# Mixing two of four batches as seven half-size products, with sums on VectorE and GpSimd

## The chip, the cores and the metric

The kernel runs on one core of one Trainium2 chip. TensorE does matrix products into PSUM, VectorE (DVE) and ScalarE (ACT) work on SBUF and PSUM, GpSimd (POOL) on SBUF alone, and SyncE (SP) issues the DMA transfers. The engines run their own instruction streams in order and wait for each other on semaphores. The metric is the device time of one execution in microseconds (us), the median over several runs.

## The reference

Four batches of 512 tokens, 512 model columns; context features of width 256, hidden width 2048.

```
query, key = ctx @ Wq.T + bq, ctx @ Wk.T + bk            # per batch, 512 x 128
A   = softmax(query @ key.T, axis=-1)                     # 512 x 512
x1  = x + tanh(g_xattn) * einsum('bln,bmn->blm', layernorm(x), A)
wu, wg, wd = ternary(W_up), ternary(W_gate), ternary(W_down)
out = x1 + tanh(g_ffn) * ((silu(layernorm(x1) @ wu.T) * (layernorm(x1) @ wg.T)) @ wd.T)
```

`layernorm` takes the mean and variance of a row; `ternary(W)` is round(W / mean|W|) clipped to -1, 0, 1, times mean|W|. The change is in the `einsum` of the third line, called the mix here: for each batch a 512 x 512 by 512 x 512 product in f32.

## The kernel before, in words

The program has an attention part (batches `b` = 0 to 3, the first 96 us) and a feed-forward part, which already multiplies in the scheme of seven half-size products. Every engine's order is written out by hand.

In batch `b`, TensorE projects the context of batch `b+1` (`project`), computes its attention energies (`energy`), transposes its softmax rows (`transpose_p`), and between these mixes batch `b` (`mix(b, i)`, `i` = 0 to 3, one for each 128 rows of tokens). A mix takes four 128 x 128 blocks of the transposed input `xT` (`xt_tile(i)`, loaded by `load_xt`) as weights and the transposed softmax `at_batch(b)` as 512 moving columns. Every f32 matmul is two records in the trace. The mix runs on the raw input. The row normalisation is put in afterwards: `stats1`/`aggregate1` on VectorE give mean and variance of the rows of `x`, `rstd1` on GpSimd turns them into the factor `tr1` (tanh(g) over the standard deviation) in four small steps, and `make_x1` on VectorE adds `tr1` times the mix to `x` and so frees the PSUM bank; there are two banks for the mix (`ps_x`).

Then `stats2`/`aggregate2` (VectorE), `rstd2` (GpSimd, two steps) and `norm_x1` (VectorE) normalise the result, and `high_t` (ScalarE) and `low_t` (VectorE) split it into two f16 parts, which DMA transposes carry to the feed-forward part. The blocks are called B11, B21, T3, T1, T2, B22 and T4; T3 to T4 are sums of blocks, that of T3 is the subtraction into `t3_sb`. In the same time ScalarE does for the next batch `bias_qk`, `exp_row`, `norm_p` (softmax rows divided by their sum) and `copy_at`, VectorE does `row_max` and `row_rsum`, and ScalarE also sums the absolute values of the weights as they land (`sum_abs`).

GpSimd's stream in this part holds the small steps only: `rstd1` and `rstd2` in the order of the tiles. A semaphore counts each kind of result: `s_r1` the rows whose `tr1` is there, `s_x1` the finished rows, `s_xm` the mixes, `s_at` the copied columns of the transposed softmax. `load_xt(b, i)` for batch 1 waits until `mix(0, i)` has read the buffer; the SP queue holds, in this order, `load_ug(1, 0)`, then `load_xt(1, 0)`, `load_ug(1, 1)`, `load_xt(1, 1)`, `load_ug(1, 2)`, `load_xt(1, 2)`, `load_ug(1, 3)`, `load_xt(1, 3)`, `load_x(2)`. `load_ug` brings a megabyte of feed-forward weights, `load_xt` a quarter of a megabyte.

## Time and profile before

| | |
|---|---|
| runs shown | 397.3, 398.37 and 398.42 us; median 398.37 |
| profiled execution, span from first to last instruction | 397.2 us |
| its own time | not listed beside the span; the median lies 1.2 us above the span |
| TensorE busy | 392.9 us, 99% of the span, granted clock 1.00 |
| VectorE, ScalarE, GpSimd busy | 309.2, 266.6, 153.5 us |
| attention part | until 96 us |

Busy time says how long an engine had an instruction in work. TensorE's records overlap, so its pace is read from the chain of waits: what ended last is followed back to what released it, and the chain's pieces follow each other without overlap. Idle time of an engine is listed with what ended it.

### The profile page before, as it was taken

What the parts mean: (1) busy time and instruction counts of PE and PEld (TensorE: products, weight loads), DVE (VectorE), ACT (ScalarE), POOL (GpSimd) and SP (SyncE); (2) the same over time, 40 slices, a digit from 0 to 9 for tenths busy, and PEclk for the clock granted to TensorE, in tenths of its full rate; (3) what the DMA queues carried; (4) which work ended last, traced back from release to release, by engine and by line L of the source; (5) the groups of instructions that cost most, each with busy time, mean ns of one, the idle gap of its engine ahead of it and who ended that gap; (6) DMA issues with size and microseconds to landing.
All of it is one profiled execution on the core that took longest, in us unless ns stands there. A gap on an engine that the chain in (4) does not pass through costs nothing.

```text
span 397.2 us, 5960 instructions
## 1 busy us (share of the span) xinstructions
PE 392.9 (99%) x1912; PEld 207.6 (52%) x1920; DVE 309.2 (78%) x457; ACT 266.6 (67%) x360; POOL 153.5 (39%) x189
## 2 busy tenths in 40 slices
PE   8999999999999999999999999999999999999997
PEld 6555545554444444444444444444445565656886
DVE  0666578988889986788897966686869989798974
ACT  3886898889779686868887863756277666654400
POOL 0224344657985004131338001535349556271000
DMA  7999949599610030030009543041500000000014
GB/s 268 410 420 390 376 173 224 141 248 217 134 70 1 2 106 2 0 106 2 1 2 212 110 90 68 0 146 70 173 37 2 0 2 1 2 0 2 0 55 160
DMA packets 43183, 43.91 MB, mean 111 GB/s; under 512 B 30992, under 2 KB 33168, under 8 KB 41104
## 3 DMA queue, kind: packets, MB, share of 16 engines
q1 hardware_dynamic: 43152, 43.53, 35.7%
q8 instruction: 16, 0.26, 0.3%
q14 instruction: 15, 0.12, 0.1%
HBM read 29.89 MB, written 6.29 MB: 91 GB/s over the span
## 4 chain that ended last, share of the span: by engine, by line
PE 93%; DVE 2%; issue 2%; ACT 1%; DMA 1%; POOL 0%; DVEq 0%; ACTq 0%; POOLq 0%
PE pair L718 23%; PE pair L720 22%; PE pair L650 14%; PE pair L792 14%; PE pair L836 11%; PE pair L625 4%; PE pair L611 3%; PE pair L636 2%; PE pair L665 1%; DMA xf<-in_first 1%; DVE xf L1467 1%; DVE x_sb L1518 0%; PE pair L669 0%; POOL xf L588 0%; DVE xf L1457 0%
## 5 line engine op out<-in xcount | busy, mean ns | idle before, releaser
L718 PE MATMUL pair<-xb_hi,w_sb 128*128 128x512 f16 x448 | 169.8, 379 | 0.2 <-DVE xf L1462 0.2
L720 PE MATMUL pair<-xb_lo,w_sb 128*128 128x512 f16 x448 | 169.8, 379 | 0.0
L718 PEld LDWEIGHTS pair<-xb_hi,w_sb 128*128 128x128 bf16 x448 | 43.8, 98 | 52.8 <-ACT xf L1145 0.9
L720 PEld LDWEIGHTS pair<-xb_lo,w_sb 128*128 128x128 bf16 x448 | 43.8, 98 | 51.1 <-issue 0.3
L1096 ACT ACTIVATE xf<-xf,small 128x512 f32<-128x512 f32 x48 | 34.6, 720 | 52.3 <-DVE xf L1462 31.6
L650 PE MATMUL pair<-sh,xt_sb 128*128 128x512 f32 (+2 forms) x160 | 57.4, 508 | 0.0
L792 PE MATMUL pair<-x_sb,sh 128*128 128x512 bf16 x248 | 55.1, 379 | 0.4
L1467 DVE SCALAR_TENSOR_TENSOR xf<-xf,small 128x512 f32<-128x512 f32 x48 | 40.0, 835 | 8.4 <-ACT xf L1096 8.4
L650 PEld LDWEIGHTS pair<-sh,xt_sb 128*128 128x128 f32 x160 | 28.0, 190 | 26.2 <-issue 22.0
L792 PEld LDWEIGHTS pair<-x_sb,sh 128*128 128x128 f16 x256 | 24.9, 98 | 30.6 <-DVE x_sb L1504 0.9
L512 POOL TENSOR_TENSOR w_sb<-w_sb 128x512 bf16<-128x512 bf16 x8 | 9.6, 1196 | 63.0 <-ACT w_sb L970 63.0
L1472 DVE TENSOR_TENSOR sh<-xf,sh 128x512 f16<-128x512 f32 x36 | 32.1, 897 | 0.7 <-ACT sh L1107 0.7
L1518 DVE SCALAR_TENSOR_TENSOR x_sb<-pair,small,x_sb 128x256 f32<-128x256 f32 (+1 forms) x57 | 25.5, 473 | 5.9 <-PE pair L836 5.4
L1504 DVE SCALAR_TENSOR_TENSOR x_sb<-pair,small,x_sb 128x512 f32<-128x512 f32 x32 | 23.9, 746 | 7.9 <-PE pair L792 7.7
L1107 ACT ACTIVATE sh<-xf 128x512 f16<-128x512 f32 x36 | 22.1, 623 | 10.5 <-DVE xf L1467 9.3
L584 POOL TENSOR_TENSOR xf<-xf 128x512 f32<-128x512 f32 x7 | 9.8, 1405 | 44.7 <-DMA xb_lo<-xf 28.7
L1457 DVE TENSOR_TENSOR xf<-pair,xf 128x1024 f32<-128x1024 f32 x16 | 19.5, 1221 | 8.8 <-PE pair L720 8.6
L1452 DVE TENSOR_TENSOR xf<-pair,xf 128x1024 f32<-128x1024 f32 x16 | 19.5, 1220 | 4.1 <-issue 1.6
L1462 DVE TENSOR_TENSOR xf<-pair,xf 128x1024 f32<-128x1024 f32 x16 | 19.5, 1219 | 4.1 <-PE pair L720 3.9
L1133 ACT ACTIVATE xf<-pair 128x1024 f32<-128x1024 f32 x16 | 16.4, 1023 | 8.1 <-PE pair L720 7.6
L1341 DVE SCALAR_TENSOR_TENSOR x_sb<-pair,small,x_sb 128x512 f32<-128x512 f32 x16 | 12.0, 747 | 11.3 <-PE pair L650 11.3
L1467 DVE SCALAR_TENSOR_TENSOR c<-c,small,pair 128x512 f32<-128x512 f32 x16 | 11.9, 743 | 10.1 <-ACT c L1096 10.1
(162 smaller groups left out, 654.6 us busy)
## 6 DMA issues: line engine op xcount, KB each, us to landing
w_sb<-in_wugT SPq DMA_DIRECT2D x8, 1024.0 KB, 11.3
xt_sb<-in_xT SPq DMA_DIRECT2D x16, 256.0 KB, 6.4
x_sb<-in_x SPq DMA_DIRECT2D x4, 1024.0 KB, 10.8
xf<-in_wdT SPq DMA_DIRECT2D x4, 1024.0 KB, 7.3
xt_sb<-in_wdT SPq DMA_DIRECT2D x4, 1024.0 KB, 5.2
x_dram<-x_sb SPq DMA_DIRECT2D x8, 256.0 KB, 2.8
out<-x_sb SPq DMA_DIRECT2D x8, 256.0 KB, 2.0
x_sb<-x_dram SPq DMA_DIRECT2D x2, 1024.0 KB, 5.7
```

The costliest lines, as they stand in the source:

```text
L650: last = pe.matmul(ps_x[i % 2][:, lo:hi], xt_tile(i)[:, k, :], at[:, k, lo:hi], start=(k == 0), stop=(k == KD - 1))
L718: pe.matmul(dst[:, m * 512:(m + 1) * 512], w[:, o:o + P], hi[:, k], start=start and k == 0, stop=False, skip_group_check=not start)
L720: last = pe.matmul(dst[:, m * 512:(m + 1) * 512], w[:, o:o + P], lo[:, k], start=False, stop=k == 1, skip_group_check=not start)
L792: ins = pe.matmul(dst, h_part(n, c, lo)[:, i * P:(i + 1) * P], t_d[:, e * DM + lo_col:e * DM + hi_col], start=first and n == units[0] and ...
L836: ins = pe.matmul(fin_bank(g, j, t), hidden(u, c, lo, min(t, NT - 1)), cols, start=first and u == units[0] and lo == 0 and not (side and t ...
L1096: act.activation(cb(n, c)[:, 0:512], src, ACT.Silu, scale=su[:, :]).then_inc(s_silu[c], 1)
L1107: act.activation(part(n, c, 0), shaped(n, c, cb(n, c)[:, 0:512]), ACT.Copy).then_inc(s_hi[c], 1)
L1452: dve.tensor_tensor(cb(n, "11"), ps_y[:, :], cb(n, "11"), ALU.add).then_inc(s_c["11"], 1)
L1467: dve.scalar_tensor_tensor(cb(n, c)[:, 0:512], cb(n, c)[:, 0:512], kap[:, :], gate, ALU.mult, ALU.mult).then_inc(s_mul[c], 1)
L1472: dve.tensor_tensor(part(n, c, 1), shaped(n, c, cb(n, c)[:, 0:512]), part(n, c, 0), ALU.subtract)\
L1504: dve.scalar_tensor_tensor(y_tile(b, i), at, c_out[:, :], y_tile(b, i), ALU.mult, ALU.add)\
L1518: dve.scalar_tensor_tensor(fin_rows(g, j, t), fin_bank(g, j, t), c_out[:, :], fin_rows(g, j, t), ALU.mult, ALU.add).then_inc(s_ef, 1)
```

## The change

In batches 0 and 1 (`NS` = 2) the mix is done as seven products of halves. The tokens are halved (`lh`), the columns of the attention matrix (`mh`) and the summed index (`nh`). `mix_product(b, j)` multiplies a 256 x 256 half-block of `xT`, or a sum of such blocks, by one of the transposed softmax: four matmuls of 256 moving columns. The sums of `xT` blocks (`x_sums`, four for each batch) are made by GpSimd, those of the softmax (`p_sums_1`, `p_sums_2`) by VectorE. Products 1, 6, 7 and 4 go into one PSUM bank and 5, 3 and 2 into the other, and each product's bank is added to `x` by `add_mixed` (two instructions of 256 columns) before the next product of that bank may start. `norm_x1` of these two batches moves from VectorE to GpSimd, GpSimd's small steps take two tiles at once (`rstd1_two`, five steps; `rstd2_two`, two steps), and `xT` of batch 1 gets a home of its own, so that its loads wait for nothing. The subtraction for T3 moves in VectorE's stream from the end of batch 1 to the first tile of batch 2. Batches 2 and 3 are mixed as before. Not shown: `stats2` and the counts on the semaphores are adapted, and `rows_in` and `rows_out` are `stats1` with `aggregate1` for one tile and `stats2` with `aggregate2` for two.

```diff
+        def xt_home(b):
+            return xb_lo[:, 1024:5120].bitcast(F32) if b == 1 else xt_flat
+        def xt_tile(b, i):
+            return xt_home(b)[:, i * KD * P:(i + 1) * KD * P].rearrange("p (k t) -> p k t", k=KD)
...
+        MIX = (1, 5, 6, 3, 7, 2, 4)
+        MIX_TO = {1: (0, 0), 5: (1, 1), 6: (0, 1), 3: (0, 1), 7: (1, 1), 2: (0, 0), 4: (1, 0)}
+        MIX_BEFORE = {2: 1, 3: 6, 7: 5}
+        XA = {1: (0, 0), 2: (0, 1), 4: (1, 1), 5: 0, 6: 1, 3: 2, 7: 3}
+        PB = {1: (0, 0), 2: (1, 0), 3: (1, 1), 5: 0, 6: 1, 7: 2, 4: 3}
...
+        def x_sum(b, k):
+            home = xf[:, 6144:8192] if b == 0 else xb_hi[:, 1024:5120].bitcast(F32)
+            return home[:, k * 512:(k + 1) * 512].rearrange("p (i s) -> p i s", i=2)
...
+        def mix_bank(j):
+            return ps_x[0 if j in (1, 6, 7, 4) else 1]
+        def mixed(b, j):
+            return 7 * b + MIX.index(j) + 1
+        def added(b, j):
+            return 14 * b + 2 * MIX.index(j) + 2
...
             def load_xt(b, i):
-                if b > 0:
-                    sp.wait_ge(s_xm, (b - 1) * NT + i + 1)
-                sp.dma_start(xt_tile(i), xT[b, i]).then_inc(d_xt[i], 16)
+                if b == 2:
+                    sp.wait_ge(s_mp, 7)
+                elif b == 3:
+                    sp.wait_ge(s_xm, i + 1)
+                sp.dma_start(xt_tile(b, i), xT[b, i]).then_inc(xt_in(b, i)[0], 16)
...
             def load_down(c):
+                if c == 1:
+                    sp.wait_ge(s_mp, 7)
...
+            def rstd1_two(b, h):
+                g, two = b * NT + 2 * h, slice(2 * h, 2 * h + 2)
+                t = tr1[:, b % 2 * NT + 2 * h:b % 2 * NT + 2 * h + 2]
+                hold(pool, s_ln1, g + 2)
+                step(pool.tensor_scalar(ve1[:, two], mv1[:, two, 1], LN_EPS, 1.0, ALU.add, ALU.mult))
+                step(pool.tensor_tensor(r1[:, two], ve1[:, two], mhalf, ALU.pow))
+                step(pool.tensor_scalar(t, r1[:, two], tanh_sb[:, 0:1], 1.0, ALU.mult, ALU.mult))
+                step(pool.tensor_tensor(km1[:, g:g + 2], mv1[:, two, 0], t, ALU.mult))
+                pool.tensor_scalar(km1[:, g:g + 2], km1[:, g:g + 2], -1.0, 0.0, ALU.mult, ALU.add).then_inc(s_r1, 2)
...
+            def x_sums(b):
+                for i in range(NT):
+                    pool.wait_ge(*xt_in(b, i))
+                pool.tensor_tensor(x_sum(b, 0), x_quarter(b, 1, 0), x_quarter(b, 1, 1), ALU.add).then_inc(s_ss, 1)
+                hold(pool, s_ss, 4 * b + 1)
+                pool.tensor_tensor(x_sum(b, 1), x_sum(b, 0), x_quarter(b, 0, 0), ALU.subtract).then_inc(s_ss, 1)
+                hold(pool, s_ss, 4 * b + 2)
+                pool.tensor_tensor(x_sum(b, 2), x_quarter(b, 0, 1), x_sum(b, 1), ALU.subtract).then_inc(s_ss, 1)
+                pool.tensor_tensor(x_sum(b, 3), x_quarter(b, 0, 0), x_quarter(b, 1, 0), ALU.subtract).then_inc(s_ss, 1)
+            def norm_x1(b, i):
+                hold(pool, s_r2, b * NT + i + 1)
+                g = b * NT + i
+                pool.tensor_scalar(xn_tile(b, i), rows(x_tile(b, i)), mv2[:, g, 0:1], r2[:, g:g + 1],
+                                   ALU.subtract, ALU.mult).then_inc(s_x2p, 1)
...
-            rstd1(0, 0)
-            rstd1(0, 1)
-            for b in range(NB - 1):
+            x_sums(0)
+            rstd1_two(0, 0)
+            rstd1_two(0, 1)
+            x_sums(1)
+            rstd1_two(1, 0)
+            rstd2_two(0, 0)
+            norm_x1(0, 0)
+            norm_x1(0, 1)
+            rstd1_two(1, 1)
+            rstd2_two(0, 1)
+            norm_x1(0, 2)
+            norm_x1(0, 3)
+            rstd1(2, 0)
+            rstd1(2, 1)
+            for h in range(2):
+                rstd2_two(1, h)
+                norm_x1(1, 2 * h)
+                norm_x1(1, 2 * h + 1)
...
+            def mix_product(b, j):
+                if j == 1:
+                    pe.wait_ge(s_at, b * NT + 2)
+                    pe.wait_ge(*xt_in(b, 0))
+                    pe.wait_ge(*xt_in(b, 1))
+                    if b > 0:
+                        pe.wait_ge(s_xe, 14 * b)
+                elif j != 5:
+                    pe.wait_ge(s_xe, added(b, {6: 1, 7: 6, 4: 7, 3: 5, 2: 3}[j]))
+                a, t = XA[j], PB[j]
+                if j in (5, 6, 3, 7):
+                    pe.wait_ge(s_ss, 4 * b + a + 1)
+                if j in (5, 6, 7, 4):
+                    pe.wait_ge(s_ts, 4 * b + t + 1)
+                left = x_sum(b, a) if j in (5, 6, 3, 7) else x_quarter(b, *a)
+                right = p_sum(b, t) if j in (5, 6, 7, 4) else p_quarter(b, *t)
+                for i in range(2):
+                    for k in range(2):
+                        last = pe.matmul(mix_bank(j)[:, i * 256:(i + 1) * 256], left[:, i, k * P:(k + 1) * P], right[:, k, :],
+                                         start=j in (1, 5, 2) and i == 0 and k == 0, stop=k == 1, skip_group_check=True)
+                last.then_inc(s_mp, 1)
...
+                if b < NS:
+                    mix_product(b, 1)
+                    energy(b + 1, 0)
+                    energy(b + 1, 1)
+                    mix_product(b, 5)
+                    mix_product(b, 6)
+                    transpose_p(b + 1, 0)
+                    energy(b + 1, 2)
+                    mix_product(b, 3)
+                    mix_product(b, 7)
+                    if b == 1:
+                        pe.wait_ge(s_qk, 5)
+                        total(0, 2 * NABS, 2 * NABS, ps_q)
+                    transpose_p(b + 1, 1)
+                    energy(b + 1, 3)
+                    mix_product(b, 2)
+                    transpose_p(b + 1, NT - 2)
+                    mix_product(b, 4)
+                    continue
...
+            def p_sums_1(b):
+                hold(dve, s_at, b * NT + NT)
+                dve.tensor_tensor(p_sum(b, 0), p_quarter(b, 0, 1), p_quarter(b, 0, 0), ALU.subtract).then_inc(s_ts, 1)
+                hold(dve, s_ts, 4 * b + 1)
+                dve.tensor_tensor(p_sum(b, 1), p_quarter(b, 1, 1), p_sum(b, 0), ALU.subtract).then_inc(s_ts, 1)
+            def p_sums_2(b):
+                dve.tensor_tensor(p_sum(b, 2), p_quarter(b, 1, 1), p_quarter(b, 0, 1), ALU.subtract).then_inc(s_ts, 1)
+                hold(dve, s_ts, 4 * b + 2)
+                dve.tensor_tensor(p_sum(b, 3), p_quarter(b, 1, 0), p_sum(b, 1), ALU.subtract).then_inc(s_ts, 1)
+            def add_mixed(b, j):
+                lh, mh = MIX_TO[j]
+                hold(dve, s_r1, b * NT + 2 * lh + 2)
+                for i in range(2):
+                    if j in MIX_BEFORE:
+                        hold(dve, s_xe, added(b, MIX_BEFORE[j]))
+                    cols = x_tile(b, 2 * lh + i)[:, mh * 256:(mh + 1) * 256]
+                    dve.wait_ge(s_mp, mixed(b, j))
+                    dve.scalar_tensor_tensor(cols, mix_bank(j)[:, i * 256:(i + 1) * 256], tr1_of(b, 2 * lh + i), cols,
+                                             ALU.mult, ALU.add).then_inc(s_xe, 1)
...
-            for i in range(2):
+            for i in range(NT):
                 mark = stats1(0, i)
                 aggregate1(0, i, mark)
...
+            for b in range(NS):
+                p_sums_1(b)
+                add_mixed(b, 1)
+                row_max(b + 1, 0)
+                row_max(b + 1, 1)
+                p_sums_2(b)
+                row_rsum(b + 1, 0)
+                row_rsum(b + 1, 1)
+                add_mixed(b, 5)
+                rows_in(b + 1, 0)
+                add_mixed(b, 6)
+                row_max(b + 1, 2)
+                rows_in(b + 1, 1)
+                add_mixed(b, 3)
+                row_rsum(b + 1, 2)
+                add_mixed(b, 7)
+                if b == 1:
+                    weight_scale(0, 2, ps_q, 0)
+                row_max(b + 1, 3)
+                if b == 0:
+                    rows_in(1, 2)
+                else:
+                    low_t(0, "B11", xf_half(0, 0))
+                add_mixed(b, 2)
+                row_rsum(b + 1, 3)
+                rows_out(b, 0)
+                add_mixed(b, 4)
+                rows_out(b, 1)
+                if b == 0:
+                    rows_in(1, 3)
+                else:
+                    low_t(0, "B21", xf_half(0, 1))
...
-                    if b == 1:
-                        if i == 2:
-                            weight_scale(0, 2, ps_q, 0)
-                            low_t(0, "B11", xf_half(0, 0))
-                        if i == 3:
-                            low_t(0, "B21", xf_half(0, 1))
-                            hold(dve, s_x2n, 2 * NT)
-                            dve.tensor_tensor(t3_sb, xf_half(1, 1), xf_half(1, 0), ALU.subtract).then_inc(s_t3, 1)
                     if b == 2:
                         if i == 0:
+                            hold(dve, s_x2p, 2 * NT)
+                            dve.tensor_tensor(t3_sb, xf_half(1, 1), xf_half(1, 0), ALU.subtract).then_inc(s_t3, 1)
                             hold(dve, s_t3, 1)
                             dve.tensor_tensor(xf_half(1, 0), xf_half(1, 0), xf_half(0, 0), ALU.subtract)\
```

GpSimd's stream at the end of batch 0 and in batch 1. Before, it holds small steps alone; L505 and L506 are `rstd2`, L497 to L500 `rstd1` of one tile:

```order
L505 TENSOR_SCALAR small<-small 128x1
L506 TENSOR_TENSOR small<-small 128x1
L497 TENSOR_SCALAR small<-small 128x1
L498 TENSOR_TENSOR small<-small 128x1
L499 TENSOR_TENSOR small<-small 128x1
L500 TENSOR_SCALAR small<-small 128x1
```

Now, with L573 to L578 the sums of batch 1's `xT`, L558 to L562 `rstd1_two`, L567 and L568 `rstd2_two` of batch 0 and L583 `norm_x1`:

```order
L573 TENSOR_TENSOR xb_hi<-xb_lo 128x512
L575 TENSOR_TENSOR xb_hi<-xb_hi,xb_lo 128x512
L577 TENSOR_TENSOR xb_hi<-xb_lo,xb_hi 128x512
L578 TENSOR_TENSOR xb_hi<-xb_lo 128x512
L558 TENSOR_SCALAR small<-small 128x2
L559 TENSOR_TENSOR small<-small 128x2
L560 TENSOR_SCALAR small<-small 128x2
L561 TENSOR_TENSOR small<-small 128x2
L562 TENSOR_SCALAR small<-small 128x2
L567 TENSOR_SCALAR small<-small 128x2
L568 TENSOR_TENSOR small<-small 128x2
L583 TENSOR_SCALAR xf<-x_sb,small 128x2x256 x2
```

Both `rstd1_two(1, 0)` and the finishing of batch 0 now stand behind the four sums, and `rstd1_two(1, 1)` stands behind the two `norm_x1`.

TensorE's stream in batch 1. Before (L650 `mix`, L625 `energy`, L636 `transpose_p`, L657 `total`):

```order
L650 MATMUL pair<-sh,xt_sb 128x384 x4
L650 MATMUL pair<-sh,xt_sb 128x128 x4
L625 MATMUL pair<-sh 128x512 x2
L650 MATMUL pair<-sh,xt_sb 128x512 x4
L636 MATMUL pair<-early,sh 128x128 x4
L625 MATMUL pair<-sh 128x512
L650 MATMUL pair<-sh,xt_sb 128x512 x4
L657 MATMUL pair<-small,early 128x8
```

Now (L775 `mix_product`, L725 `energy`, L736 `transpose_p`, L782 `total`):

```order
L775 MATMUL pair<-sh,xb_lo 128x256 x4
L725 MATMUL pair<-sh 128x512 x2
L775 MATMUL pair<-xf,xb_hi 128x256 x8
L736 MATMUL pair<-early,sh 128x128 x4
L725 MATMUL pair<-sh 128x512
L775 MATMUL pair<-sh,xb_hi 128x256 x4
L775 MATMUL pair<-xf,xb_hi 128x256 x4
L782 MATMUL pair<-small,early 128x8
```

Two products (5 and 6, the row with x8) now stand ahead of the first transposes, where one mix of the same length stood.

VectorE's stream around the first tile of batch 2. Before (L1427 the subtraction for T3, L1341 `make_x1`, L1359 `norm_x1`, L1431 the subtraction for T1):

```order
L1377 TENSOR_TENSOR xb_lo<-xf,xb_hi 128x1024
L1427 TENSOR_TENSOR t_sb<-xf 128x1024
L1341 SCALAR_TENSOR_TENSOR x_sb<-pair,small,x_sb 128x512
L1346 BN_STATS small<-x_sb 128x6
L1319 TENSOR_REDUCE small<-pair 128x1 x2
```

Now (L1633 the subtraction for T3, L1482 `make_x1`, L1527 `norm_x1`, L1635 that for T1):

```order
L1527 TENSOR_SCALAR xf<-x_sb,small 128x2x256
L1633 TENSOR_TENSOR t_sb<-xf 128x1024
L1635 TENSOR_TENSOR xf<-xf 128x1024
L1482 SCALAR_TENSOR_TENSOR x_sb<-pair,small,x_sb 128x512
L1513 BN_STATS small<-x_sb 128x6
```

The subtraction for T3 has moved from ahead of batch 2's first `make_x1` to between its first and its second.

## Rows read from the trace of the kernel before

**Rows 1.** Page, part 1: busy us (share), x instructions, of each engine.

```profile
PE 392.9 (99%) x1912; PEld 207.6 (52%) x1920; DVE 309.2 (78%) x457; ACT 266.6 (67%) x360; POOL 153.5 (39%) x189
```

**Rows 2.** Chain of waits, 0 to 130 us: start us, us, what.

```profile
3.95 3.38 PE pair L665 x8
7.33 1.73 PE pair L669 x8
...
18.07 3.47 PE pair L650 x16
21.54 1.72 PE pair L625 x4
23.26 3.43 PE pair L650 x8
26.70 0.44 PE pair L636 x4
...
40.47 3.47 PE pair L650 x16
...
66.51 1.72 PE pair L625 x4
```

**Rows 3.** Timeline of ScalarE: start us, us, engine line operation, [idle before <-releaser].

```profile
21.72 1.91 ACT L934 ACTIVATE xb_lo<-w_sb 128x2048 f16<-128x2048 f32 x1 [1.03 <-DMA w_sb<-in_wugT]
...
23.82 0.69 ACT L948 ACTIVATE sh<-pair,small 128x512 f32<-128x512 f32 x1
...
25.16 1.33 ACT L953 ACTIVATE sh<-sh,small 128x512 f32<-128x512 f32 x2
...
101.83 1.01 ACT L1145 ACTIVATE xf<-pair 128x1024 f32<-128x1024 f32 x1
```

**Rows 4.** Timeline of SyncE's DMA issues, `load_ug(1, 3)`: start us, us, line.

```profile
31.83 0.43 SPq L351 DMA_DIRECT2D w_sb<-in_wugT  x1
```

**Rows 5.** DMA issues between 31.8 and 32.4 us: KB, us from issue to landing.

```profile
w_sb<-in_wugT SPq DMA_DIRECT2D x1, 1024.0 KB, 8.6
```

**Rows 6.** Busy time 18 to 40 us by engine; last: clock, DMA share, GB/s.

```profile
18.00:40.00 22.00, 22.00 (x73) 11.42 (x72) 13.90 (x32) 16.66 (x26) 8.94 (x28) 1.00 1.01 405
```

**Rows 7.** Timeline of GpSimd's small steps: one `rstd1`, one `rstd2`.

```profile
16.80 0.19 POOL L497 TENSOR_SCALAR small<-small 128x1 f32<-128x1 f32 x1 [15.20 <-DVE small L1336]
17.14 0.56 POOL L498 TENSOR_TENSOR small<-small 128x1 f32<-128x1 f32 x1
17.84 0.19 POOL L499 TENSOR_TENSOR small<-small 128x1 f32<-128x1 f32 x1
18.20 0.27 POOL L500 TENSOR_SCALAR small<-small 128x1 f32<-128x1 f32 x1 [0.18 <-POOL small L499]
...
24.56 0.19 POOL L505 TENSOR_SCALAR small<-small 128x1 f32<-128x1 f32 x1 [4.34 <-DVE small L1352]
24.90 0.55 POOL L506 TENSOR_TENSOR small<-small 128x1 f32<-128x1 f32 x1
```

**Rows 8.** Single lines: ns min/median/max, first and last start us, shapes.

```profile
L584 POOL TENSOR_TENSOR xf<-xf x7: 1266/1273/1710, 245.4 to 347.3; 128x512 f32<-128x512 f32 x7
L1472 DVE TENSOR_TENSOR sh<-xf,sh x36: 674/681/1698, 108.3 to 377.9; 128x512 f16<-128x512 f32 x36
L1518 DVE SCALAR_TENSOR_TENSOR x_sb<-pair,small,x_sb x57: 350/476/484, 304.8 to 394.7; 128x256 f32<-128x256 f32 x55, 128x128 f32<-128x128 f32 x2
```

**Rows 9.** VectorE 0 to 125 us, by shape: xcount | busy us, mean ns | idle.

```profile
L1319 DVE TENSOR_REDUCE small<-pair 128x1 f32<-128x512 f32 x16 | 10.6, 679 | 1.4 <-PE pair L625 1.4
...
L1359 DVE TENSOR_SCALAR xf<-x_sb,small 128x512 f32<-128x512 f32 x12 | 6.5, 546 | 0.9 <-POOL small L506 0.9
```

**Rows 10.** Timeline of VectorE from batch 2's first to second `make_x1`.

```profile
66.55 0.75 DVE L1341 SCALAR_TENSOR_TENSOR x_sb<-pair,small,x_sb 128x512 f32<-128x512 f32 x1 [0.46 <-PE pair L650]
...
71.03 1.22 DVE L1431 TENSOR_TENSOR xf<-xf 128x1024 f32<-128x1024 f32 x1
72.17 0.74 DVE L1341 SCALAR_TENSOR_TENSOR x_sb<-pair,small,x_sb 128x512 f32<-128x512 f32 x1
```

More of the change, by code:

```diff
@@ L113, in gated_block_kernel @@
         d_xt = [sem(f"d_xt{i}") for i in range(NT)]
+        d_xu = [sem(f"d_xu{i}") for i in range(NT)]
         d_w = [[sem(f"d_w{m}{c}") for c in range(NABS)] for m in range(3)]
@@ L144, in gated_block_kernel @@
         s_half = sem("s_half")
+        s_ss, s_ts, s_mp, s_xe, s_x2p = (sem(n) for n in ("s_ss", "s_ts", "s_mp", "s_xe", "s_x2p"))
         s_dt, s_ev, s_shift = sem("s_dt"), sem("s_ev"), sem("s_shift")
@@ new lines, in rstd2_two @@
+            def rstd2_two(b, h):
+                two, own = slice(2 * h, 2 * h + 2), slice(b * NT + 2 * h, b * NT + 2 * h + 2)
+                hold(pool, s_ln2, b * NT + 2 * h + 2)
+                step(pool.tensor_scalar(ve2[:, two], mv2[:, own, 1], LN_EPS, 1.0 / XS ** 2, ALU.add, ALU.mult))
+                pool.tensor_tensor(r2[:, own], ve2[:, two], mhalf, ALU.pow).then_inc(s_r2, 2)
+            def x_sums(b):
[7 more added lines that the diff above has]
+                pool.tensor_tensor(x_sum(b, 3), x_quarter(b, 0, 0), x_quarter(b, 1, 0), ALU.subtract).then_inc(s_ss, 1)
@@ L526, in _ @@
             pool.wait_ge(s_const, 4)
-            rstd1(0, 0)
-            rstd1(0, 1)
-            for b in range(NB - 1):
+            x_sums(0)
[16 more added lines that the diff above has]
+                norm_x1(1, 2 * h + 1)
+            for b in range(NS, NB - 1):
                 for i in range(NT):
@@ L692, in _ @@
                     mix(b, i)
-                    if b == 1 and i == 2:
-                        pe.wait_ge(s_qk, 5)
-                        total(0, 2 * NABS, 2 * NABS, ps_q)
                     if last:
@@ L1166, in sign_down @@
                 act.wait_ge(d_spill, 16 * 8)
[L1167 removed]
+                act.wait_ge(s_x2n, 2 * NT if c > 1 else NT)
                 act.activation(t_d[:, c * ACOLS:(c + 1) * ACOLS], xt_flat[:, :], ACT.Sign, bias=nmagic).then_inc(s_tda, 1)
```

85 lines of the change are left out of this document (56 added, 29 removed).

## The prediction, as put on record before the changed kernel ran

> **What bounds the kernel now.** I read the page's busy times first: TensorE is busy 99% of the span and VectorE 78% [rows 1]. The chain of waits then shows that until the feed-forward part it is TensorE's own stream without a gap, so a microsecond taken from TensorE there is one gained, and a microsecond in which it must wait is one lost, as long as no other engine sets the pace. In the chain a full mix tile takes 3.43 us, the first of a batch 3.47, two energies 1.72 and a transposed tile 0.44 [rows 2]. The other views (timelines of ScalarE, GpSimd and SyncE, DMA issues) I read for what the new waits hang on.
>
> **What TensorE saves.** Before, a batch's mix is 3.47 + 3 x 3.43 = 13.76 us. A product is four matmuls of 256 columns, as many columns as the two energies of 512, so 1.72 us; seven make 12.04. The price of more weight loads for the same columns is at most what the first tile pays over the others for doubling its loads, 0.04 us [rows 2]. Saved: 1.72 us a batch, 3.44 in all.
>
> **Batch 0.** Product 1 runs from 18.07. The two energies and products 5 and 6 follow to 18.07 + 4 x 1.72 = 24.95. Their operands are there: GpSimd's sums of this batch are made while it was idle before (its first row is at 16.80 with 15.20 us idle [rows 7]), VectorE's two softmax sums cost 0.68 each, additions of 256 columns 0.48 each [rows 8]. Next come the transposes of the next batch's first softmax tile. They need ScalarE's `exp_row` and `norm_p`. The exponential starts at 23.82, behind the absolute sum that waited for a weight load, and the two `norm_p` are at 25.16 for 1.33 us [rows 3], the first done near 25.9. That load does not move. Before, the transposes stood at 26.70 [rows 2] and the wait was covered; now TensorE waits 25.9 - 24.95 = 0.95 us. Later products of this batch find their banks added and free by the same additions. Batch 1's mix thus starts at 40.47 - 1.72 + 0.95 = 39.7.
>
> **Batch 1: where I see the loss.** GpSimd must make the sums of `xT` before `rstd1_two(1, 0)`, and these wait for all four tiles. Their loads are issued sooner than before, but still behind `load_ug(1, 3)`. That megabyte was issued at 31.83 and landed 8.6 us later, at 40.4 [rows 4, 5]; the DMA engines were full from 18 to 40 us (share 1.01, 405 GB/s [rows 6]), and the bytes ahead of it are the same, so it can't land sooner. The last `xT` tile adds 0.26 MB / 0.405 = 0.6 us: 41.0. Then:
> - four f32 sums on GpSimd. Its row of that form is 1.27 us at best, 1.71 at most [rows 8]; VectorE will mostly stand still, so I take 1.27 and two hand-overs: 5.2 us, to 46.2;
> - `rstd1_two`: one `rstd1` runs from 16.80 to 18.47 in four steps with gaps of 0.15 to 0.18 [rows 7]; a fifth step of 0.19 with its gap makes 2.05: `s_r1` reaches 6 at 48.25;
> - VectorE's `add_mixed(1, 1)` waits for that: two additions, to 49.15, and product 6 can start at 49.2.
>
> TensorE: product 1 from 39.7, energies to 43.15, product 5 (its sum is there at 41.0 + 1.27 = 42.3) to 44.9. **It waits 49.2 - 44.9 = 4.3 us.**
>
> Behind the blocked addition on VectorE stand the next batch's `row_max`, the second softmax sums and `row_rsum`, and ScalarE waits for these. Two maxima of 0.68 [rows 9] follow from 49.1, the sums end at 51.5, the reciprocal at 51.6, `norm_p` (half of the 1.33 [rows 3]) at 52.3. Product 6 ends at 50.9: **1.4 us more** before the transposes. They and an energy (0.44 + 0.86) end at 53.65. Product 3 needs `add_mixed(1, 5)`, which needs `rstd1_two(1, 1)`, which stands behind `rstd2_two` (24.56 to 25.45, 0.9 us [rows 7]) and two `norm_x1` on GpSimd. No row shows that operation there: 0.55 from VectorE's row [rows 9] and 1.27 from GpSimd's two-input row [rows 8] bound it. I take 1.0, nearer the same engine's row. That gives 48.25 + 0.9 + 2.0 + 2.05 = 53.2, the additions end at 54.1: **0.5 us more** (nothing at 0.55, 1.0 at 1.27). From here TensorE is behind everything else: ScalarE's two absolute sums of the weights, which its `norm_p` are followed by, end before `total` needs them.
>
> The Trainium skill ("GPSIMD Engine Reference", Engine selection) says that two-input elementwise work is about twice as slow there as on VectorE and single-input work about as fast. The trace agrees on the first (1.27 against 0.68). By the second the 0.5 us would fall away and the sum be half a microsecond less; no run here shows it yet.
>
> **Batch 2 and on.** VectorE loses four `norm_x1` of 0.55 a batch in 0 and 1, worth nothing, since it waits there. But the subtraction for T3, 1.22 us like its twin for T1 [rows 10], moves between batch 2's first two `make_x1`. There VectorE sets its own pace: the first `make_x1` still waited 0.46 us for TensorE, the second, at 72.17, for nothing [rows 10]. TensorE meets that lag at the start of the feed-forward part, where its third product waits for ScalarE's copy that ends at 102.84 [rows 3], itself behind VectorE's last sums. I count the full 1.22. The DMA transposes behind it move with it.
>
> **The sum.** -1.72 + 0.95 - 1.72 + 4.3 + 1.4 + 0.5 + 1.22 = +4.9 us. The profiled execution has a span of 397.2, the median of the runs is 398.37, 1.2 above it; nothing of the change lies outside the span. So 397.2 + 4.9 + 1.2 = **403.3**, own range 401.5 to 405.
>
> **The rivals.**
> 1. *The clock falls in the wait.* At the start the eight L665 pieces take 3.38 us and the eight L669 pieces, with the same columns, 1.73 [rows 2]: TensorE, after a first idle stretch, ran at half pace, as at the lower of its two levels. Later it never stands that long: its idle time in the whole span is 397.2 - 392.9 = 4.3 us [rows 1]. If it happens again at 44.9, product 6 takes 3.4 instead of 1.7 us, of which 1.4 is covered by the wait for the transposes, and energy and product 3 may be slow too, 2.6 us: +0.3 to +2.9, so 403.6 to 406.2, middle 404.9. The Trainium skill ("TensorE: Matmul & The Clock Gate", Why this matters for your kernels) warns against idle gaps between bursts of matmuls for this reason; it speaks against the change.
> 2. *GpSimd and VectorE slow each other.* Two-input rows reach 1.71 on GpSimd and 1.70 on VectorE against medians of 1.27 and 0.68 [rows 8]. If all four sums take 1.71, the block grows by 1.8 us: 405.1. Against it: VectorE is idle then.
> 3. *The block is not there: gain.* If `s_r1` reached 6 by about 43.5, before the product's own end lets the additions start, 4.3, 1.4 and 0.5 vanish: 403.3 - 6.2 = 397.1. It would take `xT` landing near 36.5, ahead of 1 MB in the same queue. Each microsecond of earlier landing gives one back; the sign turns at 4.9 us.
>
> **How the numbers follow.** What a measurement here can tell from no change is about 0.3%, 1.2 us. Forecast 0.50, rival 1 0.22, rival 2 0.18, rival 3 0.10, the last half above and half below 397.2. The likeliest is the forecast, 403.3. Eight in ten: leaving out rival 3 and the far end of 1 gives 400.8 to 406.2, which holds the bounds of `norm_x1` (402.8 and 403.8) and of T3's 1.22 counted at nothing (402.1). Slower 0.88, within 0.3% 0.06, faster 0.06.
>
> **What would show it.** In the profile after: a product at 1.72 us; GpSimd's first batch-1 sum starting at 41.0 with DMA as releaser and the four lasting 5.2; TensorE idle 4.3 us near 45 with VectorE as releaser, then 1.4 and 0.5; batch 2's first energies at 66.51 + 3.7 = 70.2 instead of 66.51, the feed-forward part 4.9 later than before. Wrong it would be if the last `xT` tile lands before 38, if GpSimd's sums take under 1.1 or over 1.7 us each, if products take clearly more than 1.72 because weight loads show, or if VectorE absorbs the moved subtraction.

## The result, and the profile after

The changed kernel takes **410.0 us** (median of 4 runs, 408.6 to 410.7) against 398.1 of the kernel before, run beside it (397.3 to 398.4): ratio 1.0297, 95% interval 1.0271 to 1.0322. It is slower by about 12 us. The direction is the predicted one; 403.3 and the range up to 406.2 are not. The profiled execution took 410.68 us with a span of 408.9, so 1.8 us lie outside the span; the 1.2 of the prediction set the span of one execution against the median of others. Over the whole span the granted clock of the four was 0.987, 0.987, 0.992 and 0.996, at 410.68, 410.6, 409.4 and 408.59 us.

The page of the changed kernel answers to [rows 1]: TensorE has hardly more busy time than before and 11.7 us more of span around it. The last row is the granted clock in 40 slices of 10.2 us, in tenths: the fifth and sixth (41 to 61 us) show 8 and 6. The kernel before has no such dip; its clock was 1.00.

```profile
PE 393.7 (96%) x1944; PEld 216.5 (53%) x1952; DVE 317.5 (78%) x477; ACT 267.4 (65%) x360; POOL 174.4 (43%) x185
...
PEclk9999869999999999999999999999999999999999
```

TensorE's timeline from batch 1 to the feed-forward part (start us, us, engine line operation, [idle before <-releaser]; L775 is `mix_product`, L736 the transposes, L725 the energies, L752 `mix`, L859 the feed-forward part). The rows of before for the two mixes are in [rows 2].

```profile
38.91 1.89 PE L775 MATMUL pair<-sh,xb_lo 128*128 128x256 f32 x8
...
42.40 1.99 PE L775 MATMUL pair<-xf,xb_hi 128*128 128x256 f32 x8
49.69 3.78 PE L775 MATMUL pair<-xf,xb_hi 128*128 128x256 f32 x8 [5.29 <-DVE x_sb L1505]
53.26 1.06 PE L736 MATMUL pair<-early,sh 128*128 128x128 f32 x4
54.11 1.64 PE L725 MATMUL pair<-sh 128*128 128x512 f32 x2
57.76 2.84 PE L775 MATMUL pair<-sh,xb_hi 128*128 128x256 f32 x8 [2.01 <-DVE x_sb L1505]
60.39 2.77 PE L775 MATMUL pair<-xf,xb_hi 128*128 128x256 f32 x8
...
72.24 3.63 PE L752 MATMUL pair<-sh,xt_sb 128*128 128x384 f32 x16
...
88.26 0.66 PE L736 MATMUL pair<-early,sh 128*128 128x128 f32 x4 [1.20 <-ACT sh L1094]
93.29 0.66 PE L736 MATMUL pair<-early,sh 128*128 128x128 f32 x4 [0.94 <-ACT sh L1094]
...
107.78 0.38 PE L859 MATMUL pair<-xb_hi,w_sb 128*128 128x512 f16 x1
```

GpSimd's timeline shows what VectorE waited for (L573 to L578 `x_sums`, L558 to L562 `rstd1_two`, L567 and L568 `rstd2_two`, L583 `norm_x1`).

```profile
41.08 1.27 POOL L573 TENSOR_TENSOR xb_hi<-xb_lo 128x512 f32<-128x512 f32 x1 [18.14 <-DMA xb_lo<-in_xT]
...
45.13 1.26 POOL L578 TENSOR_TENSOR xb_hi<-xb_lo 128x512 f32<-128x512 f32 x1
46.47 0.19 POOL L558 TENSOR_SCALAR small<-small 128x2 f32<-128x2 f32 x1
...
50.32 4.14 POOL L583 TENSOR_SCALAR xf<-x_sb,small 128x512 f32<-128x512 f32 x2 [0.19 <-POOL small L568]
...
56.54 0.19 POOL L562 TENSOR_SCALAR small<-small 128x2 f32<-128x2 f32 x1 [0.17 <-POOL small L561]
```

The five small operations from 46.47 end at 48.65: up to there this is the predicted chain, 0.4 us late. Then comes a row that was not: two `norm_x1` take 4.14 us, 2.07 each, where 1.0 had been taken. The second `rstd1_two` ends at 56.73 instead of the predicted 53.2, and product 3 starts at 57.76.

TensorE's clock, in windows (us, busy us and count, granted clock, DMA share, GB/s): after the wait of 5.29 us it is at 0.50 of full speed, the lower of its two levels, and product 6 has 3.57 us to the next row instead of 1.73.

```profile
48.00:50.00 2.00, 0.31 (x1) 0.63 1.03 384
50.00:52.00 2.00, 2.00 (x6) 0.50 1.06 390
52.00:54.00 2.00, 2.00 (x8) 0.50 0.66 239
...
60.00:64.00 4.00, 4.00 (x17) 0.73 0.00 0
```

Where the time went, from the starts in TensorE's timelines of both kernels (batch 0's mix at 17.91 and 17.43, batch 1's at 40.31 and 38.91, batch 2's at 62.88 and 72.24, feed-forward at 95.84 and 107.78):

| stretch | before | after | difference |
|---|---|---|---|
| to batch 0's mix | 17.91 | 17.43 | -0.48 |
| batch 0's mix to batch 1's | 22.40 | 21.48 | -0.92 |
| batch 1's mix to batch 2's | 22.57 | 33.33 | +10.76 |
| batch 2's mix to feed-forward | 32.96 | 35.54 | +2.58 |
| feed-forward to the end | 301.36 | 301.12 | -0.24 |

In batch 2 VectorE is the late one. It waits for GpSimd, which normalises batch 1 until 80.16, and makes the T3 subtraction (L1633) right behind it:

```profile
81.25 0.55 DVE L1527 TENSOR_SCALAR xf<-x_sb,small 128x512 f32<-128x512 f32 x1 [1.27 <-POOL small L590]
81.71 1.22 DVE L1633 TENSOR_TENSOR t_sb<-xf 128x1024 f32<-128x1024 f32 x1
...
84.17 0.75 DVE L1482 SCALAR_TENSOR_TENSOR x_sb<-pair,small,x_sb 128x512 f32<-128x512 f32 x1
```

Its second `make_x1` of batch 2 is 8.25 us behind the first (75.92); in [rows 10] it was 5.62. The 2.6 us between them are the T3 subtraction (1.22) and the wait behind GpSimd (1.27).

### The profile page after: what moved, and what is told of

Same layout as the page of the kernel before. It is cut to its first block, busy times and chain, and to the rows that moved or that the text cites. A ratio compares the mean times of both kernels' runs of the same rounds, so it can differ in the third digit from the quotient of the medians.

```text
span 408.9 us, 6058 instructions
## 1 busy us (share of the span) xinstructions
PE 393.7 (96%) x1944; PEld 216.5 (53%) x1952; DVE 317.5 (78%) x477; ACT 267.4 (65%) x360; POOL 174.4 (43%) x185
## 4 chain that ended last, share of the span: by engine, by line
PE 75%; DVE 6%; DMA 5%; issue 5%; POOL 5%; ACT 2%; SPq 1%; DVEq 0%; POOLq 0%; ACTq 0%
PE pair L859 22%; PE pair L861 22%; PE pair L933 13%; PE pair L977 11%; DMA xb_lo<-in_xT 5%; PE pair L752 3%; POOL xf L583 2%; PE pair L775 1%; DVE small L1460 1%; DMA xf<-in_first 1%; DVE xf L1671 1%; ACT sh L1089 1%; SPq L400 1%; POOL small L568 1%; PE pair L790 0%
## 5 line engine op out<-in xcount | busy, mean ns | idle before, releaser
L859 PE MATMUL pair<-xb_hi,w_sb 128*128 128x512 f16 x448 | 169.8, 379 | 0.2 <-DVE xf L1666 0.2
L859 PEld LDWEIGHTS pair<-xb_hi,w_sb 128*128 128x128 bf16 x448 | 43.8, 98 | 52.5 <-DVE xf L1666 0.6
L1708 DVE SCALAR_TENSOR_TENSOR x_sb<-pair,small,x_sb 128x512 f32<-128x512 f32 x32 | 23.9, 747 | 7.8 <-PE pair L933 7.6
L752 PE MATMUL pair<-sh,xt_sb 128*128 128x512 f32 (+2 forms) x80 | 28.6, 508 | 0.0
L1505 DVE SCALAR_TENSOR_TENSOR x_sb<-pair,small,x_sb 128x256 f32<-128x256 f32 x28 | 12.3, 479 | 15.1 <-POOL small L562 13.0
L752 PEld LDWEIGHTS pair<-sh,xt_sb 128*128 128x128 f32 x80 | 13.9, 190 | 12.6 <-issue 10.5
L1089 ACT ACTIVATE sh<-pair,small 128x512 f32<-128x512 f32 x16 | 10.9, 683 | 14.7 <-DVE small L1460 14.6
```

The source lines that it names most:

```text
L752: last = pe.matmul(ps_x[i % 2][:, lo:hi], xt_tile(b, i)[:, k, :], at[:, k, lo:hi], start=(k == 0), stop=(k == KD - 1))
L859: pe.matmul(dst[:, m * 512:(m + 1) * 512], w[:, o:o + P], hi[:, k], start=start and k == 0, stop=False, skip_group_check=not start)
L1708: dve.scalar_tensor_tensor(y_tile(b, i), at, c_out[:, :], y_tile(b, i), ALU.mult, ALU.add)\
```

## The experiments

Theory A: the loss is GpSimd's queue (late landing, sums, 2.07-us norms, all in front of a step that VectorE needs). Theory B: the lower clock carries it. Theory C: the seven products bring waits of their own. "Expected" is what was written down before each run. Times are medians; the kernel before, run beside each, was at 397.8 to 398.2.

### Order, norms, clock and loads, one at a time

**e1_steps_first.** GpSimd makes both steps of batch 1 ahead of the sums.

```diff
-            x_sums(1)
             rstd1_two(1, 0)
+            rstd1_two(1, 1)
+            x_sums(1)
             rstd2_two(0, 0)
             norm_x1(0, 0)
             norm_x1(0, 1)
-            rstd1_two(1, 1)
```

> Both rstd1_two of batch 1 stand ahead of the four sums on GpSimd; nothing else changes. Theory A (what costs the time is GpSimd's order: tr1 of batch 1 stands behind the sums and the two-microsecond normalisations): TensorE's waits of 5.3 and 2.0 us before products 6 and 3 vanish, and with them the fall of the clock; granted clock 1.0 throughout. What stays is the moved subtraction for T3 and the late normalisations: about 400, 9 to 10 us less than the changed kernel. Theory B (the clock's fall is the larger part by itself): gives the same here. Theory C (the seven products cost waits of their own, whatever the order): products 6 and 3 still wait 3 us or more, over 404.

Measured: 405.99, ratio 1.0199 [1.0182, 1.0216]. Product 6 and product 3 no longer wait. But the sums now start at 43.28, behind a step whose statistics are ready only at 40, and product 5 waits for the first; and the norms, still 4.14 us a pair, are late for ScalarE, which needs the four of batch 0 before it goes on to batch 2's softmax. TensorE's timeline:

```profile
44.60 3.72 PE L775 MATMUL pair<-xf,xb_hi 128*128 128x256 f32 x16 [1.20 <-POOL xb_hi L573]
...
64.15 1.11 PE L736 MATMUL pair<-early,sh 128*128 128x128 f32 x4 [4.00 <-ACT sh L1094]
65.05 3.06 PE L711 MATMUL pair<-sh,early 128*128 128x512 f32 x4
```

Four microseconds are won, where the order alone was to win nine to ten: the queue is still too long.

**e2_norms_on_dve.** The norms of batches 0 and 1 back on VectorE, those of batch 0's first two rows right behind `rows_in(1, 3)`.

```diff
                 if b == 0:
                     rows_in(1, 3)
...
+                norm_x1(b, 0)
+                norm_x1(b, 1)
```

> Only norm_x1 of batches 0 and 1 goes back to VectorE, GpSimd's order is otherwise that of the changed kernel. Theory A: product 6 still waits 5.3 us, the clock still falls, the second wait (product 3) goes from 2.0 us to nothing and GpSimd's later steps come in time: about 406, 3 to 4 us less. If the normalisations on GpSimd were the main cost: under 402. If they were covered: 409 to 410.

Measured: 408.85, ratio 1.0273 [1.0253, 1.0293]: a miss. These two norms wait on VectorE for `rstd2_two(0, 0)`, which stands behind the sums on GpSimd, and `p_sums_1(1)` stands behind them: VectorE idles 10.15 us, and product 5 waits 8.34.

```profile
50.19 1.00 DVE L1521 TENSOR_SCALAR xf<-x_sb,small 128x512 f32<-128x512 f32 x2 [10.15 <-POOL small L568]
```

My edit made a wait of its own; it says nothing on the price of the norms. e5 does it over.

**e3_filler_in_waits.** Five unread matmuls (ten records) before product 6 and five before product 3 of batch 1, to keep TensorE busy in its waits.

```diff
                     mix_product(b, 5)
+                    if b == 1:
+                        for _ in range(5):
+                            pe.matmul(ps_q, ones[:, :], k_sb, start=True, stop=True)
                     mix_product(b, 6)
```

> Ten matmuls that nobody reads, 0.86 us each, fill TensorE's two waits in batch 1 (five ahead of product 6, five ahead of product 3), so that it does not stand idle; no wait is taken away. Theory A: the waits end when they did, granted clock stays at 1.0, and only products 3 and 7, which follow the second wait, take 1.72 instead of 2.6 us: 1.8 us less than the changed kernel, about 408. Theory B: product 6, the transposes, the energy and both products all come earlier, 4.8 us less, about 405. If the clock falls anyway, nothing changes or it is slower.

Measured: 409.79, ratio 1.0294 [1.0278, 1.031]; the clock stays at 1.00. TensorE's timeline (L821, L827 are the fillers):

```profile
44.51 4.45 PE L821 MATMUL pair<-sh,early 128*128 128x512 f32 x10
49.65 1.99 PE L775 MATMUL pair<-xf,xb_hi 128*128 128x256 f32 x8 [0.68 <-DVE x_sb L1511]
53.06 0.66 PE L736 MATMUL pair<-early,sh 128*128 128x128 f32 x4 [1.42 <-ACT sh L1100]
...
54.41 4.45 PE L827 MATMUL pair<-sh,early 128*128 128x512 f32 x10
58.70 1.89 PE L775 MATMUL pair<-sh,xb_hi 128*128 128x256 f32 x8
```

At full clock product 6 still starts at 49.65, and the transposes wait 1.42, where the prediction had 49.2 and 1.4. The fillers were one too many before product 3: the additions were made at 57.7, it started at 58.70. From there it runs at full speed: the next transposes are 3.60 us behind it, in the changed kernel 5.39. So the slow clock costs 1.8 us behind product 3, of which this run gave 0.9 back to its own fillers. Before product 3 it costs nothing, because GpSimd sets that time. Theory B holds for 1.8 of 12 us in the profiled execution. This is read from the two traces; the medians, 409.79 and 410.0, don't show it. It isn't in every execution either: see e11.

**e4_xt_loads_first.** SyncE issues the four `xT` loads of batch 1 ahead of the last three loads of weights.

```diff
             for i in range(NT):
                 load_xt(1, i)
-                if i < 3:
-                    load_ug(1, i + 1)
+            for i in range(3):
+                load_ug(1, i + 1)
```

> The four xT loads of batch 1 are issued ahead of the last three weight loads; GpSimd's order stays. Theory A: the last xT tile lands near 33 instead of 41 us, the sums end near 38.8 and rstd1_two near 41, product 6 waits for nothing, product 3 about 2 us for the second rstd1_two behind the normalisations; about 402, 7 to 8 us less. Theory C: over 405. If the landing was not what held GpSimd: no change.

Measured: 403.16, ratio 1.0123 [1.0102, 1.0145]. GpSimd's first sum starts at 33.80 instead of 41.08, product 6 doesn't wait, product 3 waits 2.60 behind the norms. With GpSimd's queue as it is, the late landing costs 6.8 us.

### Both causes mended

**e5_norms_on_dve_later.** The norms on VectorE, those of batch 0 behind `row_max(2, 2)`, those of batch 1 at its end.

```diff
                 row_max(b + 1, 2)
+                if b == 1:
+                    for i in range(NT):
+                        norm_x1(0, i)
```

> The changed kernel with the row normalisation of batches 0 and 1 on VectorE again, this time behind batch 1's products 5 and 6 (so that nothing that a product waits for stands behind it), and GpSimd left with the token sums and the small steps. Token sums still start when the last xT tile lands (about 41). Theory A (what the change costs is GpSimd's queue: the late token sums and the 2.07-us norms): product 6 still waits about 5.3 us; rstd1_two(1,1) is done at about 52 in place of 56.7, so product 3 waits for nothing (2.0 us less, and its half clock); the 1.20-us wait of the transposes in batch 2 goes, the 0.94-us one stays: about 406.5. Theory B (the lower clock carries the loss): the clock still falls, 409 or more. Theory C (the seven products bring waits of their own, whoever normalises): 409 or more.

Measured: 405.52, ratio 1.0193 [1.0163, 1.0223]. Product 6 waits the same 5.29, product 3 and the first transposes of batch 2 for nothing, the last for 0.81. With the loads as they are, the norms' place costs 4.5 us, the slow clock behind product 3 included: that product starts at 54.62 here and runs at full speed.

**e6_xt_first_norms_dve** is e4 and e5 together.

> The kernel before plus products, with the xT loads of batch 1 ahead of the last three weight loads, and the norms on VectorE. Theory A: of the 403.2 with the loads moved alone, 2.6 (wait before product 3), 1.7 (that product's half clock) and 1.2 (transposes of batch 2) go; the 0.93-us wait stays, since the T3 subtraction still stands in batch 2: about 397.7. Theory C: waits of 2 us or more remain in the two batches with seven products: 400 or more.

Measured: **397.68**, ratio 0.9998 [0.9986, 1.001], as expected. The 12.3 us are gone, 11.3 of them the two single effects added. Theory C is out as stated: no wait of 2 us or more is left. The waits that the view of TensorE lists (L730 the transposes, L769 `mix_product` here):

```profile
15.48 0.66 PE L730 MATMUL pair<-early,sh 128*128 128x128 f32 x4 [0.41 <-DVE sh L1551]
16.89 0.66 PE L730 MATMUL pair<-early,sh 128*128 128x128 f32 x4 [0.76 <-DVE sh L1551]
...
53.37 1.99 PE L769 MATMUL pair<-sh,xb_lo 128*128 128x256 f32 x8 [0.16 <-DVE x_sb L1499]
...
81.05 0.66 PE L730 MATMUL pair<-early,sh 128*128 128x128 f32 x4 [0.80 <-ACT sh L1088]
```

**e7_xt_first_norms_dve_t3** is e6 with the T3 subtraction back at the end of batch 1.

```diff
+                    hold(dve, s_x2p, 2 * NT)
+                    dve.tensor_tensor(t3_sb, xf_half(1, 1), xf_half(1, 0), ALU.subtract).then_inc(s_t3, 1)
```

> As the run with the loads first and the norms on VectorE, and the T3 subtraction back at the end of batch 1. Theory A: the last wait of batch 2 (0.93) goes too: about 396.8, and no wait of TensorE over 0.5 us after 40 us. Rival: VectorE's 1.22 us for the subtraction is only shifted and costs the same at the end of batch 1 (make_x1 of batch 2 late): no difference from the run without it, 397.7.

Measured: 398.27, ratio 1.0006 [0.9995, 1.0017]: the rival. The wait of 0.80 shrinks to 0.29 and one of 0.33 appears at 70.58; VectorE has the same to do in either place.

**e8_order_norms_dve_t3** moves no load: `rstd1_two(1, 0)`, sums, `rstd1_two(1, 1)` on GpSimd, norms and T3 as in e7.

> No DMA moved: the loads as in the changed kernel, but GpSimd in the order rstd1_two(1,0), token sums, rstd1_two(1,1), norms on VectorE, T3 subtraction at the end of batch 1. Theory A (the late landing costs only through what is queued behind the sums): product 6 waits for nothing, product 3 about 1.3 us (sums end at 46.4, the step at 48.5, its rows at 49.5 for a product due at 48.2), batch 2 no wait: 398 to 399. Rival (the late landing costs by itself, since the sums are needed then): 400 or more.

Measured: 401.69, ratio 1.0096 [1.0077, 1.0115]. Product 6 doesn't wait; product 3 waits 2.38, not 1.3, and it and product 7 behind it are slow (2.30 and 2.95 us):

```profile
50.42 2.50 PE L769 MATMUL pair<-sh,xb_hi 128*128 128x256 f32 x8 [2.38 <-DVE x_sb L1499]
```

So the order of GpSimd's queue and the norms take 8.3 of the 12 us off. Against e7, which has the loads moved and the norms and T3 in the same places (GpSimd's order differs), 3.4 stay with the late landing: the rival, 400 or more.

### One part alone, and what the seven products don't give

**e12_before_norms_on_gpsimd.** The kernel before, eight products, with `norm_x1` of batches 0 and 1 on GpSimd behind the steps of its row tile.

```diff
                     else:
                         rstd1(b + 1, i + 2 - NT)
+                    if b < 2:
+                        norm_x1(b, i)
```

Not shown: VectorE waits for the matching norm before it writes new statistics over the old ones. The trace shows no idle time of VectorE there.

> One part of the change alone: the kernel before, with the row normalisation of batches 0 and 1 on GpSimd (2.07 us each behind the steps of its row tile), eight products as they were. Theory A: the last row of batch 1 is normalised at about 67.3 (its sums at 62, step 1.3, next step 1.9, norm 2.07), so the T3 subtraction on VectorE, at 64.9 before, waits 2.4 us and with it the row tiles of batch 2: 399.5 to 400.5. Rival (8 of these are hidden behind TensorE): 398.

Measured: 402.91, ratio 1.0111 [1.0084, 1.0137], more than expected. GpSimd's last norm runs from 66.43 to 68.50, not to 67.3, and the T3 subtraction on VectorE waits for it. VectorE's row, and in the second fence TensorE's:

```profile
68.61 1.23 DVE L1437 TENSOR_TENSOR t_sb<-xf 128x1024 f32<-128x1024 f32 x1 [5.13 <-POOL xf L511]
```

```profile
74.09 0.66 PE L644 MATMUL pair<-early,sh 128*128 128x128 f32 x4 [2.56 <-ACT sh L961]
74.58 1.68 PE L633 MATMUL pair<-sh 128*128 128x512 f32 x2
76.05 4.68 PE L658 MATMUL pair<-sh,xt_sb 128*128 128x512 f32 x8
```

TensorE waits 2.56 us, near the expected 2.4. The rest is the clock: the energy behind the transposes takes 1.47 us to the next row (0.86 before), the mix tile 4.52 (3.43 before), 1.7 together. The norms on GpSimd cost over 3 us without any seven-product mix. This is with the T3 subtraction at its old place right behind them; the changed kernel has it one tile later, so it isn't their price there.

**e9_sums_after_rows.** e6, and in batch 0 GpSimd makes one sum and waits with the others until VectorE has normalised the P rows, the softmax rows of batch 0 that VectorE divides by their sums before the first mix (Theory D: the two engines exclude each other). **e10_sums_after_rows_t3** is the same with T3 moved as in e7.

```diff
+            x_sums(0, 1)
+            pool.wait_ge(s_pn0, 3)
+            x_sums(0, 2)
             rstd1_two(0, 0)
             rstd1_two(0, 1)
+            x_sums(0, 3)
```

> The kernel with the loads first and the norms on VectorE (397.7), and in batch 0 GpSimd makes one token sum, then waits until VectorE has normalised the three P rows, and makes the other three behind that (one before the two rstd steps, two after). In the runs so far these three rows took 1.49, 0.64 and 1.03 us beside GpSimd's sums and 0.49, 0.48 and 0.49 in the kernel before, and TensorE waited 0.4 to 0.6 and 0.75 us for them. Theory D (an operation of VectorE on SBUF and GpSimd's two-input operations exclude each other for a whole instruction): the rows take 0.49 again, both waits go, about 1.2 us less: 396.5. Rival (the rows were slow for another reason, or the sums are then late for products 5 and 6): 397.7 or more.

> The same with the T3 subtraction back at the end of batch 1: by the pair of runs without the later sums it makes no difference, so 396.5; if VectorE's first row tiles of batch 2 are what is left, up to 0.8 us less (the transposes' last wait in batch 2): 395.7.

Measured: 397.66, ratio 0.9992 [0.9982, 1.0002], and 397.91, ratio 1.0 [0.9987, 1.0014]. VectorE's P rows of batch 0 in e7 (first fence) and in e9 (second), L1551 and L1557 being the same line of the program:

```profile
12.73 1.49 DVE L1551 TENSOR_SCALAR sh<-sh,small 128x512 f32<-128x512 f32 x1
...
16.00 1.03 DVE L1551 TENSOR_SCALAR sh<-sh,small 128x512 f32<-128x512 f32 x1
```

```profile
12.20 0.49 DVE L1557 TENSOR_SCALAR sh<-sh,small 128x512 f32<-128x512 f32 x1
...
14.46 0.49 DVE L1557 TENSOR_SCALAR sh<-sh,small 128x512 f32<-128x512 f32 x1
...
22.61 1.75 DVE L1494 TENSOR_TENSOR xf<-sh,xf 128x512 f32<-128x512 f32 x1
```

The mechanism is as expected: in e9 both waits of batch 0 are gone, in e10 one of 0.35 is left. The total doesn't gain. The delayed sums now lie beside `p_sums_2` (1.75 for 0.68), and the transposes behind that wait 0.97.

**e11_changed_sums_after_rows** is the changed kernel with this edit alone.

> The changed kernel with this edit of batch 0 alone. Theory A: batch 0's time is worth nothing in the changed kernel, since the wait before product 6 of batch 1 is ended by a load that lands at 41: batch 1 starts 1 us earlier and the wait grows by as much, 409.5 to 410. Rival (the loss in batch 0 counts by itself): 408.8.

Measured: 410.55, ratio 1.0325 [1.0294, 1.0356]: no gain. But the run didn't put its expectation to the test. VectorE's rows take 0.49 again and batch 0's mix starts at 17.23, 0.2 earlier; then ScalarE's weight load lets it start at 21.31 (21.03 in the changed kernel), the transposes wait 1.02 instead of 0.54, and batch 1's mix starts at 39.18, not earlier than 38.91. That batch 0's time is worth nothing rests on other rows: product 6 starts 8.6 us behind the first token sum, whenever TensorE comes (41.08 to 49.69 in the changed kernel, 41.30 to 49.91 here, 41.03 to 49.65 in e3 with batch 1's mix at 39.34).

This trace shows something else (L781 is `mix_product`). Product 3 waits 3.14 us, longer than the 2.01 of the changed kernel, and yet it and product 7 run at full speed:

```profile
57.98 1.99 PE L781 MATMUL pair<-sh,xb_hi 128*128 128x256 f32 x8 [3.14 <-DVE x_sb L1511]
59.81 1.89 PE L781 MATMUL pair<-xf,xb_hi 128*128 128x256 f32 x8
```

The next transposes are 3.70 us behind product 3, against 5.39 in the changed kernel. So the 1.8 us of the clock are in one execution of this program and not in the other.

**e13_no_overlap**: as e9, the last two sums behind `p_sums_2` (`pool.wait_ge(s_ts, 4)` ahead of them). **e14_no_overlap_t3**: T3 moved as well.

> Like the run in which GpSimd makes the last three token sums of batch 0 behind the P rows (397.7), and the last two of them behind VectorE's p_sums_2 too. There VectorE's second operation of p_sums_2 took 1.75 us beside a sum of 1.70 (0.69 alone) and the transposes behind it waited 0.97. Theory D (the two engines exclude each other): p_sums_2 takes 0.70 each, the wait goes, product 3 waits at most 0.3 for its sum: 396.8. Rival (what the seven products lose in the early batches isn't this): 397.7.

> The same with the T3 subtraction back at the end of batch 1. By the two pairs of runs so far it makes no difference: 396.8; if the 0.80-us wait of batch 2 was what is left, 396.0.

Measured: 397.59, ratio 0.9989 [0.9973, 1.0004], and 397.84, ratio 0.9993 [0.9978, 1.0009]: no gain that these runs can tell. `p_sums_2` takes 0.68 each, but the transposes still wait, 1.08, now by ScalarE, whose absolute sum waited for a weight load as in [rows 3] (e13, ScalarE's timeline):

```profile
21.50 1.91 ACT L1076 ACTIVATE xb_lo<-w_sb 128x2048 f16<-128x2048 f32 x1 [1.36 <-DMA w_sb<-in_wugT]
```

In e14 the same load let ScalarE start at 20.93, and the wait was 0.18. Theory D is borne out by the operations and not by the total.

The busy times of the stretches answer the rest (window; PE, PEld, DVE, ACT, POOL; clock, DMA share, GB/s), first the kernel before, then e13, each from one batch's mix to the next and to the feed-forward part:

```profile
17.90:40.30 22.40, 22.40 (x73) 11.57 (x72) 14.07 (x32) 16.66 (x26) 9.34 (x28) 1.00 1.00 403
40.30:62.90 22.60, 22.60 (x76) 11.81 (x75) 14.87 (x37) 20.32 (x29) 8.44 (x23) 1.00 0.72 256
62.90:95.80 32.90, 32.90 (x107) 17.10 (x106) 28.86 (x53) 27.81 (x38) 19.49 (x39) 1.00 0.86 214
```

```profile
17.40:39.40 22.00, 20.92 (x90) 15.15 (x89) 18.51 (x47) 16.61 (x26) 11.98 (x16) 1.00 1.02 414
39.40:60.70 21.30, 21.14 (x92) 15.37 (x91) 18.76 (x47) 18.83 (x28) 8.94 (x24) 1.00 0.81 288
60.70:95.00 34.30, 33.49 (x108) 17.06 (x106) 31.03 (x59) 29.81 (x40) 19.67 (x37) 1.00 0.81 190
```

Of 3.4 us saved, batch 0 keeps 0.4 and batch 1 1.3; the third stretch, batches 2 and 3, which have no seven products, is 1.4 longer. VectorE has 8.3 us more to do in the first two stretches and 2.2 more in the third, where it was 88% busy before. Of the 1.4 there, TensorE's listed wait is 0.81 (0.63 in e14, whose stretch is as long), and the first mix tile and energies of batch 2 take 0.3 more. That VectorE's load is what eats the rest is read from these windows and not shown; no run took it away.

## Why the prediction was wrong, step by step

- **Product at 1.72, landing at 41.0, four sums 5.2, `s_r1` = 6 at 48.25:** 1.73, 41.08, 5.3, 48.65. Right, to within half a microsecond.
- **Wait before product 6, 4.3 us:** 5.29, half of the difference because TensorE came 0.5 earlier. The mechanism is as told; e4 takes 6.8 us off by moving the loads alone.
- **Transposes, 1.4 more:** not seen, as rival 1 said: the slow product 6 covers it. At full clock it is 1.42 (e3).
- **Product 3, 0.5 more: the step that failed.** "I take 1.0, nearer the same engine's row" and its upper bound 1.27 were both under the truth: 2.07 each. With two norms 2.1 over, `rstd2_two` 0.8 over (a hand-over of 0.50 and 0.70 for the power on two columns) and 0.6 over in the two steps, `rstd1_two(1, 1)` ends 3.5 late, and product 3 starts 3.6 after its predicted 54.15. A two-input row of 1.27 is no upper bound for a one-input operation of another kind.
- **Rival 1, the clock, +0.3 to +2.9:** it happened, next to the forecast and not in its place. In the profiled execution it costs 1.8, behind product 3 (e3); in that of e11 nothing there.
- **Batch 2, +1.22 for T3:** the stretch is 2.58 longer. The 1.22 is there in VectorE's rows. What was missing is GpSimd: its norms run to 80.16 and hold VectorE 1.27 us in batch 2. With the norms on VectorE, T3's place makes no difference that can be told (e6 against e7, e9 against e10, e13 against e14); with the norms on GpSimd no run moved it. "VectorE loses four `norm_x1`, worth nothing" was right only of batches 0 and 1.
- **Batch 0, -1.72 + 0.95:** the stretch gave -0.92. The one wait in it, 0.54 us, is ScalarE's behind the weight load, as told. VectorE's P rows, slowed by GpSimd's sums, lie ahead of the stretch (0.73 us of waiting). None of it counts, since the wait in batch 1 ends by the landing (8.6 us behind the first sum, see e11).
- **Rival 2, GpSimd and VectorE slow each other, +1.8:** not in batch 1, where the four sums took 1.27 each with VectorE idle, as the prediction said against it. In batch 0 it happened.
- **Rival 3:** its number, 397.1 with the block gone, supposed that only the landing was in the way. With the landing mended alone it is 403.2, with the norms too 397.7.

The sum was 4.9 and is 11.7 in the span. The landing was foreseen; what failed is the price of `norm_x1` on GpSimd and what hangs on it. Feed-forward starts 7.0 later than forecast: 3.6 product 3 late, 1.8 clock, 1.4 more in batch 2, 0.2 rest.

The Trainium skill ("GPSIMD Engine Reference", Engine selection), cited in the prediction, has one-input work on GpSimd about as fast as on VectorE. The trace disagrees for this one: 2.07 against 0.55. The measurement decides.
